# Two streams of matmuls and a lent PSUM bank: who gets bank F2 in the free windows of a period

## The reference

```python
query = split_heads(q @ w_q.T + b_q)      # 8, 16 heads, 512, 16
key = split_heads(k @ w_k.T + b_k)        # 8, 16 heads, 1601, 16
value = split_heads(v @ w_v.T + b_v)
scores = jnp.einsum('bhqd,bhkd->bhqk', query, key) / np.sqrt(D_K)
scores = jnp.where(mask == 0, jnp.float32(-1000000000.0), scores)
attn = jax.nn.softmax(scores, axis=-1)
x = jnp.einsum('bhqk,bhkd->bhqd', attn, value)
```

## Time and profile before

| | |
|---|---|
| median of 3 runs | 2822.28 us (2820.21 to 2825.11) |
| profiled execution | 2816.4 us |
| its span, first to last instruction | 2814.6 us |
| mean granted TensorE clock | 0.989 |
| one period | 302.8 us |

### The profile page before, as it was taken

The page is one execution under the profiler, slowest core; times in us unless marked ns, Lnnn a source line. Parts: engine busy times, 40 slices in busy tenths (PEclk is TensorE's granted clock), DMA queues, the critical chain, the costliest instruction groups (busy, mean ns, idle before and its releaser), DMA issues.

```text
span 2814.6 us, 39400 instructions
## 1 busy us (share of the span) xinstructions
PE 2632.1 (94%) x13626; PEld 1283.8 (46%) x13626; DVE 1729.8 (61%) x4198; ACT 1447.7 (51%) x2923; POOL 281.8 (10%) x344
## 2 busy tenths in 40 slices
PE   7878999999999999999999999999999989999998
PEld 3534433344334434443335433443444323349998
DVE  3346677577765776667666776677666768853111
ACT  2232565546554565456554656456545745663332
POOL 1200100011000200020001100020002000002221
PEclk9988999999999999999999999999999999999999
DMA  5431322423132413241232313241224023169995
GB/s 185 119 102 53 88 58 56 109 61 98 42 110 53 120 41 99 55 122 34 79 92 64 88 42 110 60 120 42 90 57 104 19 52 74 34 205 375 369 363 169
DMA packets 215140, 296.36 MB, mean 105 GB/s; under 512 B 50533, under 2 KB 180813, under 8 KB 214934
## 3 DMA queue, kind: packets, MB, share of 16 engines
q1 hardware_dynamic: 198428, 221.50, 28.1%
q0 software_dynamic: 16512, 72.32, 7.5%
HBM read 232.87 MB, written 60.50 MB: 104 GB/s over the span
## 4 chain that ended last, share of the span: by engine, by line
PE 78%; DVE 9%; ACT 6%; issue 5%; SPq 1%; DMA 1%; POOL 0%; ACTq 0%; POOLq 0%; DVEq 0%
PE PS L1616 12%; PE PS L1568 10%; PE PS L1599 10%; PE PS L1242 7%; DVE mxC L2176 6%; PE PS L1214 6%; PE PS L1751 5%; PE PS L1761 5%; PE PS L1271 3%; PE PS L1441 2%; PE PS L1338 2%; PE PS L1361 2%; ACT reg L1108 2%; PE PS L1230 2%; ACT reg L995 2%
## 5 line engine op out<-in xcount | busy, mean ns | idle before, releaser
L1108 ACT ACTIVATE reg<-PS 128x512 f32<-128x512 f32 (+1 forms) x1664 | 962.3, 598 | 946.2 <-PE PS L1599 940.0
L2176 DVE TENSOR_REDUCE mxC<-PS 128x1 f32<-128x400 f32 (+1 forms) x2048 | 1091.0, 570 | 529.4 <-PE PS L1568 513.6
L1568 PE MATMUL PS<-reg 96*128 96x400 bf16 (+1 forms) x2048 | 665.3, 339 | 51.6 <-DVE mxC L2176 20.8
L1599 PE MATMUL PS<-reg 99*128 99x512 bf16 (+1 forms) x1664 | 606.7, 384 | 23.0 <-ACT reg L1108 18.5
L1616 PE MATMUL PS<-reg 128*17 128x512 f32 (+1 forms) x3328 | 439.6, 600 | 1.1 <-DVE reg L2200 0.7
L1568 PEld LDWEIGHTS PS<-reg 96*128 96x128 bf16 x2048 | 195.2, 98 | 519.9 <-DVE mxC L2176 375.5
L1599 PEld LDWEIGHTS PS<-reg 99*128 99x128 bf16 (+1 forms) x1664 | 164.0, 100 | 351.0 <-ACT reg L1108 191.1
L1214 PE MATMUL PS<-reg 128*128 128x512 f32 (+1 forms) x512 | 209.8, 524 | 14.5 <-DVE small L1924 13.8
L1242 PE MATMUL PS<-reg 128*128 128x512 f32 (+1 forms) x416 | 211.5, 601 | 0.7 <-ACT reg L982 0.7
L1141 ACT ACTIVATE reg<-PS,reg 128x128 f32<-128x128 f32 x312 | 89.0, 368 | 197.9 <-PE PS L1751 110.4
L1751 PEld LDWEIGHTS PS<-reg 128*128 128x128 f32 x1248 | 145.0, 192 | 2.7 <-issue 0.9
(11 more groups left out here) (268 smaller groups left out, 2513.9 us busy)
## 6 DMA issues: line engine op xcount, KB each, us to landing
reg<-in_D_W SPq DMA_DIRECT2D x78, 1024.0 KB
reg<-in_A_mask POOLq DMA_DIRECT2D x32, 800.5 KB, 6.6
dramK<-reg SPq DMA_DIRECT2D x144, 100.0 KB
dramV<-reg SPq DMA_DIRECT2D x48, 272.0 KB, 3.1
reg<-in_ctxT POOLq DMA_DIRECT2D x8, 1601.0 KB, 9.7
reg<-in_ctx POOLq DMA_DIRECT2D x8, 1536.0 KB, 7.7
dramQ<-reg SPq DMA_DIRECT2D x96, 128.0 KB
reg<-dramQ SPq DMA_DIRECT2D x32, 384.0 KB, 5.8
```

Of the source, the lines that this page charges most:

```text
L1108: act.activation(pr[u % RING][0:r, :], PS[0:r, S_PLAN[NU * b + u][0], :], ACT.Exp).then_inc(a_expC, 1)
L1568: last = mm(PS[:, bank, 0:w], qs[(NG * bb + g) % 3][0:ROWS, h, t * P:(t + 1) * P], ks[g % 2][0:ROWS, h, c0:c0 + w], start=True, stop=True)
L1599: last = mm(PS[0:r, bank, :], ks[g % 2][0:STK, h, c * P:c * P + r], qs[(NG * b + g) % 3][0:STK, h, :], start=True, stop=not with_mask)
L2176: v.tensor_reduce(mxC[:, h, t, j:j + 1], PS[:, M_PLAN[bb, g, i][0], 0:M_CH[j][1]], AX.X, ALU.max).then_inc(v_mx, 1)
```

## The change

F2 leaves the ring of the pieces in the three windows and joins the ring of the scores there. `maxima_plan` gives every piece outside the last period banks 0 and 1 (0, 1 and F0 for the last period's first group, made in period 6, which had F2 as well). `score_plan` adds F2 to SB inside a window of periods 0 to 6. The waits at a window's opening move from the first F2 piece to the first F2 score, and the waits after a window are for the exp instead of the reduction. The third window starts at step 149 instead of 147. The number and order of matmuls, exps and reductions are unchanged.

```diff
--- before.py
+++ after.py
@@ -101,7 +101,7 @@
 W_PIECE, W_ROWS = (186, 218), 222
 W_END = 226
 
-SPARE = ((U_RL + 2, U_XA[0]), (U_PVB[1] + 3, U_XC[0]), (U_XC[1] + 1, NU))
+SPARE = ((U_RL + 2, U_XA[0]), (U_PVB[1] + 3, U_XC[0]), (U_XC[1] + 3, NU))
 
 
 class Ticks:
@@ -156,52 +156,48 @@
 
 def maxima_plan():
 
-    plan, spare_last, last, count = {}, {}, {}, 0
+    plan, last, count = {}, {}, 0
     for bb in range(B):
         for g in range(NG):
-            b, w = (bb, g - 1) if g else (bb - 1, NG - 1)
-            steps = [w * UN + v for v in range(UN) for _ in chunks(b, w, v)] if b >= 0 else [None] * NSC
-            for i, u in enumerate(steps):
-                ring, window = MB, None
-                if b < 0:
+            for i in range(NSC):
+                ring = MB
+                if bb == 0 and g == 0:
                     ring = MB + SB
-                elif bb == B - 1 and g:
-                    ring = MB_END[:3] if g == 1 else MB_END
-                else:
-                    if bb == B - 1:
-                        ring = MB_END[:3]
-                    window = spare_at(u)
-                    if window is not None:
-                        ring += (F2,)
+                elif bb == B - 1:
+                    ring = MB_END if g > 1 else MB_END[:3]
                 bank = min(ring, key=lambda k: last.get(k, -1))
-                opens = window is not None and bank == F2 and (b, window) not in spare_last
-                plan[bb, g, i] = bank, last.get(bank, -1) + 1, (b + 1, window) if opens else None
+                plan[bb, g, i] = bank, last.get(bank, -1) + 1
                 last[bank] = count
                 count += 1
-                if bank == F2:
-                    spare_last[b, window] = count
-    return plan, spare_last
-
-
-M_PLAN, SPARE_LAST = maxima_plan()
+    return plan
+
+
+M_PLAN = maxima_plan()
 
 
 def score_plan():
 
-    plan, last = [], {}
+    plan, spare_last, last = [], {}, {}
     for U in range(NU * B):
-        ring = SB
+        ring, window, b = SB, None, U // NU
         if U >= NU * B - UN:
             ring = SB + (F1, F0)
         elif U >= NU * (B - 1) - UN:
             ring = SB + (F1,)
+        if b < B - 1:
+            window = spare_at(U % NU)
+            if window is not None:
+                ring += (F2,)
         bank = min(ring, key=lambda k: last.get(k, -1))
-        plan.append((bank, last.get(bank, -1) + 1))
+        opens = window is not None and bank == F2 and (b, window) not in spare_last
+        plan.append((bank, last.get(bank, -1) + 1, (b + 1, window) if opens else None))
         last[bank] = U
-    return plan
-
-
-S_PLAN = score_plan()
+        if bank == F2:
+            spare_last[b, window] = U + 1
+    return plan, spare_last
+
+
+S_PLAN, SPARE_LAST = score_plan()
 
 
 def ring_a(n, i):
@@ -1396,7 +1392,7 @@
 
                 if k == 0:
                     pe.wait_ge(v_ao, NG * (e + 1))
-                    pe.wait_ge(v_mx, SPARE_LAST[e, 2])
+                    pe.wait_ge(a_expC, SPARE_LAST[e, 2])
                 else:
                     pe.wait_ge(a_aT, 2 * e + 1)
                 for t in range(QT):
@@ -1500,7 +1496,7 @@
                     if u == p.XC[k]:
                         pe.wait_ge(v_otB, 2 * n + 2)
                         if n and k == 0:
-                            pe.wait_ge(v_mx, SPARE_LAST[n - 1, 1])
+                            pe.wait_ge(a_expC, SPARE_LAST[n - 1, 1])
                         turn_x(norm_c(n), k)
                         piece()
                     if u == p.QC[k]:
@@ -1523,7 +1519,7 @@
                 for k in range(KD):
                     if u == p.XA[k]:
                         if p is LOOP and k == 0:
-                            pe.wait_ge(v_mx, SPARE_LAST[m - 2, 0])
+                            pe.wait_ge(a_expC, SPARE_LAST[m - 2, 0])
                         turn_x(norm_a(m), k)
                         piece()
                     if u == p.QG[k]:
@@ -1554,16 +1550,8 @@
                     pe.wait_ge(v_tq, 2 * B)
                 if bb == B - 1 and g == 2 and i == 0:
                     pe.wait_ge(v_rk, 2)
-                bank, before, opened = M_PLAN[bb, g, i]
+                bank, before = M_PLAN[bb, g, i]
                 past(pe, v_mx, before)
-                if opened:
-                    n, window = opened
-                    if window == 0:
-                        pe.wait_ge(v_rm, n + 1)
-                    elif window == 1:
-                        pe.wait_ge(v_otB, 2 * n + 2)
-                    else:
-                        pe.wait_ge(a_xT, 2 * norm_c(n) + 2)
                 c0, w = M_CH[j]
                 last = mm(PS[:, bank, 0:w], qs[(NG * bb + g) % 3][0:ROWS, h, t * P:(t + 1) * P],
                           ks[g % 2][0:ROWS, h, c0:c0 + w], start=True, stop=True)
@@ -1590,8 +1578,16 @@
                 if v == 0:
                     pe.wait_ge(m_loaded, 16 * (NG * b + g + 1))
                     pe.wait_ge(ks_hi[g % 2], 16 * len(KPART) * (2 * b + g // 2 + 1))
-                bank, before = S_PLAN[U]
+                bank, before, opened = S_PLAN[U]
                 past(pe, a_expC, before)
+                if opened:
+                    n, window = opened
+                    if window == 0:
+                        pe.wait_ge(v_rm, n + 1)
+                    elif window == 1:
+                        pe.wait_ge(v_otB, 2 * n + 2)
+                    else:
+                        pe.wait_ge(a_xT, 2 * norm_c(n) + 2)
                 if U == NU * (B - 1) - UN:
                     pe.wait_ge(v_tq, 2 * B)
                 if U == NU * B - UN:
```

## The result

The changed kernel takes 2846.18 us (median of four runs, 2845.62 to 2848.63) against 2821.24 us before (2815.25 to 2825.11): a ratio of 1.0092, 95% interval 1.0073 to 1.0111. It is slower by 0.9%, and 4 us from the forecast of 2850. The profiled execution took 2845.62 us (span 2843.9), 29.2 us above the one before, where the sum had 27.5.

A forecast was written before the change was run, and what follows sets the result against it. PE was taken as the path. Six periods lose 5.0 less 1.2 us each (23 us), period 6 4.5: +27.5 on 2816.4 gives 2844; the median's 5.9 us offset makes it 2850 us, 8-in-10 range 2832 to 2878.

The forecast's parts named there:

- The price of a station: Where three pieces come close together, the third waits for the first reduction on two banks: 0.44 us late at steps 167/168.
- The stations: Places in a usual period's three windows where a piece comes late: 1.6, 0.9 and 2.5 us, together 5.0 us lost.
- rival 2: Lateness is paid at every dense step, 20 places with three pieces in a usual period's windows: 2874 us; chance 12%.
- step 190: Window 2: a piece 0.40 us late, but PE then waits 1.04 us for exp_a anyway, so nothing counted.
- rival 1: Window 2: PE's waits on L1924 and ACT absorb lateness, only 0.7 of 2.5 us stays: 2837 us; chance 15%.
- Rival 3: Whole kernel: no difference, pieces have slack or gain and loss cancel: 2822 us; chance 8%.
- rival 4: Opening at step 147 and L1230 after step 166 decide, leaving a gain of 1.2 us a period: 2814 us; chance 6%.
- the finding that I quoted from the Trainium skill: Dense matmul kernel: PSUM double-buffering gave no further gain (126.6 against 125.5 us); by that the moved bank would leave 2822.
- The openings: Window 1's opening: a score now waits for L2117, 0.22 us lost; step 147: no wait for turned xC, 0.87 us earlier.
- The scores' gain: Third score bank: 0.34 us back at step 166; bounds 0 and 18.5 us in all, taken near the low end.
- hardly fall: Sign to look for in the changed trace: PE's wait at scores for exps (L1108), 18.5 us before, hardly falls.
- Period 6: Windows 0 and 1 cost 1.6 and 0.9, opening gives back some 1, DVE-bound window 2 costs 3: 4.5 us.
- rival 5: More short stops let the granted clock fall to 1.2 GHz for stretches in 20 windows: 68 us more, 2918 us; chance 2%.

The follow-up runs named there:

- e1: Changed kernel with bank F2 taken from the pieces and given to nobody (scores on two banks): 2843.38 us, ratio 1.0081 to the kernel before.
- e3: Kernel before with window 2 opening for the pieces at step 149 instead of 147 and window 1 at 132 instead of 131: 2810.30 us, ratio 0.9961.
- e8: The changed kernel timed once more without further edits, on one chip with the kernel before: 2846.64 us, ratio 1.0098.
- e9: Changed kernel with F2 given back to the pieces in period 6 only, window 2 opening there at step 149: 2841.54 us, ratio 1.0076 to the kernel before.

## Why the prediction was right, point by point

**The price of a station.** Steps 167 and 168 in the changed kernel's timeline, the same place as the earlier trace rows:

```profile
1423.62 0.51 PE L1556 MATMUL PS<-reg 96*128 96x400 bf16 x2
...
1424.00 2.68 DVE L2172 TENSOR_REDUCE mxC<-PS 128x1 f32<-128x400 f32 x5
...
1424.63 0.34 PE L1556 MATMUL PS<-reg 96*128 96x400 bf16 x1 [0.28 <-DVE mxC L2172]
```

The first reduction starts at 1424.00 and ends at 1424.57; the third piece starts at 1424.63, 0.06 later, where before it came 0.57 after the first of the two. It comes 1.01 after it now: 0.44 late, as worked out. The step after it starts 0.45 later relative to the period.

**The stations,** by the starts of the scores after each of them:

| steps | forecast | measured |
|---|---|---|
| 56 | 0.44 | 0.45 |
| 61, 62 | 0.52 | 0.53 |
| 66 | 0 | 0.00 |
| 74 | 0.22 | 0.23 |
| 76 | 0.44 | 0.46 |
| opening of window 1 | 0.22 | 0.23 |
| 132 | 0.44 | 0.45 |
| 141 | 0.22 | 0.23 |
| 147 | -0.87 | -0.85 |
| 166 | -0.34 | -0.28 |
| 168 | 0.44 | 0.45 |
| 171 to 174 | 0.44 | 0.47 |
| 178 | 0.40 | 0.41 |
| 180 | 0.44 | 0.45 |
| 183 to 186 | 0.44 | 0.47 |
| 190 | 0 | 0.00 |
| 196 to 199 | 0.34 | 0.36 |
| sum | 3.79 | 4.06 |

The rule "late once per run of reductions" held, so rival 2 (20 places) is out; and lateness of the pieces was absorbed only at step 190, so rival 1 is out too. Rival 3 (no difference) and rival 4 (the openings outweigh the pieces) are out by the interval of the ratio: the openings and step 166 gave 1.13 us a period, as forecast, but all of the pieces' loss survived. In this kernel the further bank is worth 3.47 us a period to the pieces as the kernel before opens its windows (302.83 us against 306.30 in e1, where nobody has it), and 4.87 with the openings of e3 (301.43); the finding that I quoted from the Trainium skill ("TensorE: Matmul & The Clock Gate", section "HAM oscillation — how this bites in real kernels"), of no further gain from PSUM double-buffering, doesn't carry over to it. Step 190 in the changed kernel: counted from the score of step 189, the first of these two pieces is 0.44 late and the second 0.40, as worked out, and L1226 starts when exp_a ends, as before:

```profile
1458.21 0.34 PE L1556 MATMUL PS<-reg 96*128 96x400 bf16 x1 [0.28 <-DVE mxC L2172]
...
1458.69 0.35 PE L1556 MATMUL PS<-reg 96*128 96x401 bf16 x1
...
1459.66 0.66 PE L1226 MATMUL PS<-ident,reg 128*128 128x128 f32 x4 [0.63 <-ACT reg L967]
```

Its wait is 0.63 us instead of 1.04. Step 174 behaves as the text said: the wait for the fused add and maximum is 0.77 us instead of 0.88, so only a tenth is given back.

```profile
1435.40 0.32 PE L1210 MATMUL PS<-reg 128*128 128x65 f32 x1 [0.77 <-DVE small L1920]
```

**The openings.** Step 131, where a score now stands for L2113 (L2117 before), and step 147, where no turned xC is waited for and the piece stops for its reduction instead, until 1393.49; before, it was 1.27 us:

```profile
1366.84 0.74 DVE L2113 TENSOR_SCALAR reg<-PS,bs 128x512 f32<-128x512 f32 x1
...
1367.72 0.38 PE L1595 MATMUL PS<-reg 99*128 99x512 bf16 x1 [0.89 <-DVE reg L2113]
```

```profile
1393.49 0.34 PE L1556 MATMUL PS<-reg 96*128 96x401 bf16 x1 [0.40 <-DVE mxC L2172]
```

The 0.40 us there is the wait for the reduction that used bank 1, and it was in the sum (1378.66 to 1379.06).

**The scores' gain.** Here one sign of the prediction failed: the wait for L1108 was to "hardly fall", and it fell from 18.5 to 11.4 us (with two score banks it is still 17.1 in e1). Yet only some 1.7 us (six times 0.28) became time, as the low bound that I had taken says. A place that the prediction passed over is step 66: with the third bank its score starts 0.46 us earlier, and L1292, soon behind it, then waits 0.29 us for DVE's L1982; the score of step 67 stands as if nothing had been won. At step 166, as in the earlier trace rows:

```profile
1418.98 0.82 PE L1595 MATMUL PS<-reg 99*128 99x512 bf16 x3
...
1421.42 0.19 ACT L967 ACTIVATION_READ_ACCUMULATOR reg<-reg,small 128x1 f32 x1
...
1421.66 0.66 PE L1226 MATMUL PS<-ident,reg 128*128 128x128 f32 x4
```

Three scores go in a row (0.82 us), and then L1226 waits for exp_a, whose accumulator read ends at 1421.61. The score's wait of 0.47 us has turned into a wait for ACT.

**Period 6** is the term that was mis-sized: 4.5 us forecast, 5.7 measured in the profiled execution and 4.0 in e8, the same kernel. Its stretches are steps 0 to 130, 131 to 148, 149 to 167 and 168 to 199; the last eight steps got 0.57 us shorter. Before:

```profile
2071.09:2261.82 190.73, 183.32 (x929) 79.96 (x926) 129.55 (x310) 107.98 (x214) 17.48 (x20) 1.00 0.24 59
2261.82:2287.30 25.48, 21.20 (x115) 8.58 (x114) 21.73 (x51) 10.63 (x20) 3.47 (x16) 1.00 0.13 25
2287.30:2313.98 26.68, 18.63 (x83) 5.36 (x82) 10.96 (x26) 12.71 (x24) 0.00 (x0) 0.82 0.42 113
2313.98:2340.97 26.99, 26.96 (x153) 8.56 (x152) 26.70 (x56) 17.34 (x32) 0.00 (x0) 0.99 0.23 55
```

After:

```profile
2095.14:2288.20 193.06, 184.29 (x930) 79.74 (x926) 130.83 (x312) 108.02 (x214) 17.51 (x20) 1.00 0.23 58
2288.20:2315.83 27.63, 25.18 (x115) 9.42 (x115) 20.86 (x49) 10.83 (x19) 3.33 (x16) 0.81 0.12 22
2315.83:2341.53 25.70, 18.25 (x83) 5.30 (x82) 10.96 (x26) 12.58 (x24) 0.00 (x0) 0.80 0.42 117
2341.53:2371.27 29.74, 28.55 (x153) 7.72 (x152) 27.70 (x56) 17.69 (x32) 0.00 (x0) 1.00 0.21 50
```

The last row is as forecast: 2.75 us more for the rounds (3 forecast, and the same 2.75 in e8), DVE 27.70 of 29.74 us busy instead of all of it. Between two runs of seven reductions DVE now stands idle for 0.25 or 0.26 us, eight times over, where the trace before has 58 reductions without a gap, 0.48 us apart; a round takes 3.72 us (to the next start at 2349.17), 0.33 more than seven of those:

```profile
2345.45 3.46 DVE L2172 TENSOR_REDUCE mxC<-PS 128x1 f32<-128x400 f32 x7 [0.26 <-PE PS L1556]
```

The second row grew by 2.15 us where the opening should have given some back, and there the granted clock averages 0.81 instead of 1.00: a dip to half the clock fell on a stretch where PE is needed:

```profile
2300.30:2310.50 10.20, 9.65 (x34) 2.68 (x35) 6.49 (x15) 2.88 (x5) 3.33 (x16) 0.50 0.00 0
```

A dip of some 10 us in the third stretch stands in both (0.82 and 0.80), where PE is busy for only about half of its length; the one in the second stretch is new. The third row got 0.98 us shorter. So rival 5, the clock, has a small real part, in periods 6 and 7 only. In e8, the same kernel, the period took 280.45 us instead of 282.13, and steps 131 to 148 took 25.25 instead of 27.63 at a clock of 0.93, with a dip of some 3.4 us at the same steps:

```profile
2290.74:2315.99 25.25, 22.67 (x114) 8.88 (x115) 20.71 (x49) 10.70 (x19) 3.32 (x16) 0.93 0.14 24
```

So 4.5 us was too much rather than too little for what the banks do, and what made it 5.7 was the longer dip, which the sum didn't have. That 2850 came out 4 us from the median is partly luck. The mechanism of the stations held, but how long the dip of an execution is moves period 6 by 1.7 us (5.7 against 4.0), and whole executions of the changed kernel spread over 3 to 5 us. No run separates what sets the place or the length of a dip.

**The medians.** The profiled executions differ by 29.2 us and the medians by 24.9 (27.5 in e8). I had moved the sum by the 5.9 us between the one profiled execution and the median of three; the later runs of before (medians of 2819.2 to 2819.8 over nine to eleven) say that the true offset is nearer 3, and the forecast of 2850 was too high by that.

## What to carry to other kernels

In this kernel the bank was worth more to the stream whose consumer is slow and whose matmuls come in bursts: three in a row on two banks wait for one whole read of the first, 0.57 us here, whatever the averages say. Price such a burst as end of the first read, plus the 0.06 us measured here, less the time at which the third matmul would start, once for each burst, and ask at each whether the next wait is for an engine that the lateness doesn't reach. When a bank is lent at a fixed step, look whether the first borrower is the one that waits for its former owner: moving two opening steps made the old kernel 10 us faster, and lending the bank to the scores where the pieces don't need it added only 0.26 us a period.

## What the runs showed of the hardware

**Reductions overlap.** One takes 0.57 us, but in a full queue they start 0.48 us apart (ten in 4.89 us); with 200 columns one takes 0.36.

**The granted clock dips up to the first microseconds of period 0 and in periods 6 and 7, and not between.** In periods 1 to 5 of all traces it stays at 1.00. A dip to 0.50 of some 7 or 10 us stands at step 164 of period 6 in every trace; others come and go, between kernels and between two executions of one. Of two executions of nearly the same kernel, the stretch from 7 to 22 us has a mean clock of 1.00 in the changed kernel

```profile
7.00:22.00 15.00, 8.11 (x18) 3.97 (x17) 3.93 (x14) 1.79 (x3) 1.95 (x3) 1.00 1.02 402
```

and of 0.66 in e9

```profile
7.00:22.00 15.00, 8.11 (x18) 4.14 (x17) 3.93 (x14) 1.79 (x3) 1.93 (x3) 0.66 1.01 394
```

and the first score of period 0 comes 3.7 us later in the second (262.8 instead of 259.1 us). That this dip is the cause is not shown: e8 has 1.00 there too, and its first score comes at 261.8. Whole executions spread by about as much, while periods 1, 3, 4 and 5 of one execution agree to 0.1 us (but for one period 0.4 us longer in one short-reduction trace): differences of 0.1% between two kernels can be read in a period's row and not in two medians.

**Lateness can vanish behind a DMA.** Period 2 takes 303.45 us before, 0.6 more than the others, and 306.90 in the changed kernel, like the others. ACT's copy of the projected k (L989) waits at step 64 for the store of an earlier piece. Before, the timeline shows ACT idle for 1.25 us there in period 2 and for 0.43 in period 3, both ended by that DMA; in the changed kernel, later by a microsecond, ACT doesn't wait for it in period 2. In e1, as late but with two score banks, period 2 is still 0.25 us longer than the others (306.55 against 306.30), so the third score bank may take part in it.
